# Routed expert layer, decayed attention, routed expert layer: the first layer's tiles divided 4 and 4 steps instead of 5 and 3

## The reference, cut to what matters

```python
x = x + 0.5 * ffn(layernorm(x), ...)
x = x + attn(layernorm(x), ...)
x = x + 0.5 * ffn(layernorm(x), ...)

def ffn(x, Wr, br, W1, b1, W2, b2):     # 8 experts, hidden width 512
    expert = argmax(x @ Wr.T + br)
    h = relu(x @ W1[expert].T + b1[expert])
    return h @ W2[expert].T + b2[expert]

def attn(x, ...):                       # 16 heads of 8, chunks of 128 tokens
    q, k, v = silu(x @ Wq), silu(x @ Wk), silu(x @ Wv)
    # per chunk: o = (q k^T * mask) v + lam_q * (q kv);  kv = lam_c * kv + (k * lam_k)^T v
    o = normalise(o) * gamma + beta
    return (o * sigmoid(x @ Wg1 @ Wg2)) @ Wo
```

## Time and profile before

| what | before |
|---|---|
| median of 3 runs | 430.17 us (429.95 to 430.38) |
| the profiled execution | 426.96 us |
| its span | 424.9 us |
| PE busy | 358.1 us, 84% |
| DVE busy | 288.4 us, 68% |
| POOL busy | 284.5 us, 67% |
| ACT busy | 192.1 us, 45% |
| DMA moved | 54.00 MB |

### The profile page before, as it was taken

One profiled execution on the slowest core, in us unless ns is written; L12 is line 12 of the kernel. 1 busy time (PEld: TensorE's weight loads), 2 busy tenths in 40 slices (PEclk: granted clock), 3 DMA queues, 4 the chain that ended last, 5 costly groups with the idle time before them and its releaser, 6 DMA issues.

```text
span 424.9 us, 10262 instructions
## 1 busy us (share of the span) xinstructions
PE 358.1 (84%) x2508; PEld 319.2 (75%) x2508; DVE 288.4 (68%) x995; ACT 192.1 (45%) x608; POOL 284.5 (67%) x303
## 2 busy tenths in 40 slices
PE   6788989999989979879897978855589999999920
PEld 6787879999978767667676766645489899999910
DVE  4872675444563698999898989897665676566510
ACT  5723745565546322535456363240455435555500
POOL 0027774754885999998989777620777777777770
PEclk9555999999999979998999999986599999999975
DMA  8938686887761000001010110102687846767410
GB/s 231 349 107 270 194 240 186 223 190 231 219 188 41 21 0 19 2 19 57 7 62 2 50 49 2 50 2 71 191 238 246 199 139 193 228 198 199 134 35 0
DMA packets 41303, 54.00 MB, mean 127 GB/s; under 512 B 6212, under 2 KB 25818, under 8 KB 40992
## 3 DMA queue, kind: packets, MB, share of 16 engines
q1 hardware_dynamic: 34640, 39.97, 29.9%
q0 software_dynamic: 6176, 13.26, 13.0%
q10 hardware_dynamic: 432, 0.14, 0.2%
HBM read 41.93 MB, written 12.32 MB: 128 GB/s over the span
## 4 chain that ended last, share of the span: by engine, by line
PE 55%; POOL 15%; DVE 11%; issue 10%; ACT 3%; DMA 2%; DVEq 1%; POOLq 0%; ACTq 0%
PE bank L1226 17%; PE bank L1216 17%; POOL outer_all L451 5%; PE bank L1272 4%; POOL rows L410 4%; PE bank L1176 4%; PE bank L1170 3%; POOL qS L459 3%; PE bank L1254 3%; PE bank L1208 2%; PE bank L1192 2%; POOL out_x L429 2%; PE bank L1290 2%; DVE st L702 1%; POOL kd L438 1%
## 5 line engine op out<-in xcount | busy, mean ns | idle before, releaser
L396 POOL DMA_INDIRECT ring<-rows_d,token_in x92 | 87.8, 955 | 78.0 <-DVE token_in L884 50.9
L1216 PE MATMUL bank<-slot_xT,w_ring 128*128 128x128 f32 x736 | 103.9, 283 | 4.9 <-DVE hT_b L924 4.0
L1216 PEld LDWEIGHTS bank<-slot_xT,w_ring 128*128 128x128 f32 x736 | 93.6, 197 | 8.6 <-DVE hT_b L924 6.0
L924 DVE TENSOR_SCALAR hT_b<-bank,b_cur 128x128 f32<-128x128 f32 x184 | 56.0, 346 | 38.2 <-PE bank L1216 32.6
L451 POOL TENSOR_TENSOR outer_all<-qkv 128x512 f32<-128x512 f32 x64 | 66.4, 1063 | 4.0 <-ACT qkv L577 4.0
L1272 PE MATMUL bank<-outer_all,decay_sb 128*128 128x256 f32 x256 | 68.0, 392 | 1.0 <-DVE qS L966 1.0
L560 ACT ACTIVATE hT_a<-bank,b_cur 128x128 f32<-128x128 f32 x184 | 57.3, 363 | 12.4 <-PE bank L1216 11.5
L1226 PE MATMUL bank<-w_sb,hT_a 128*128 x368 | 59.2, 284 | 3.4 <-DVE ring L937 0.6
L1272 PEld LDWEIGHTS bank<-outer_all,decay_sb 128*128 128x128 f32 x256 | 48.3, 197 | 16.6 <-issue 5.4
L1226 PE MATMUL bank<-w_sb,hT_b 128*128 x368 | 56.5, 276 | 0.0
L429 POOL DMA_INDIRECT out_x<-ring,token_out x46 | 46.1, 1002 | 14.0 <-issue 11.9
(11 more groups left out here) (127 smaller groups left out, 498.8 us busy)
## 6 DMA issues: line engine op xcount, KB each, us to landing
w_ring<-in_w1t SPq DMA_DIRECT2D x92, 256.0 KB
rows_d<-rows SPq DMA_DIRECT2D x8, 512.0 KB, 2.9
y_d<-kd SPq DMA_DIRECT2D x46, 64.0 KB
rows<-in_x SPq DMA_DIRECT2D x8, 256.0 KB, 5.9
w_sb<-in_w2t SPq DMA_DIRECT2D x1, 2048.0 KB, 8.8
rows_d<-rows SPq DMA_DIRECT2D x8, 256.0 KB, 3.7
ring<-rows_d,token_in POOLq DMA_INDIRECT x92, 4.0
decay_sb<-in_decay SPq DMA_DIRECT2D x1, 1024.0 KB, 8.1
```

The source lines that it names most:

```text
L396: pool.indirect_dma_start(n_in_ring(G) if layer_of(G) == 0 else in_ring(G), None, rows_d[u], bass.IndirectOffsetOnAxis(ap=token_in[u][:, j ...
L924: last = nc.vector.tensor_scalar(hT_b[G % 2][:, f * P:(f + 1) * P], bank_b[:, f * P:(f + 1) * P], b1_cur[G % 2][:, 2 + f:3 + f], 0.0, ALU. ...
L1216: last = mm(to[:, f * P:(f + 1) * P], w1_ring[G % W1_BUFS][:, (2 * half + f) * P:(2 * half + f + 1) * P], slot_xT[G % 2][:, :], start=True ...
```

## The change

The first layer's units get 4 and 4 steps: 16 tiles and 23 slots each. What follows from that is written out by hand: ACT's list of normalises between the routing copies, SP's store hooks (steps 4 to 7 at 6, 8, 10, 12), and GpSimd's order in attention's first five turns, with 16 fetches in place of 12, a possible fourth one in a turn ahead of half-sum 4, and four sums in place of three. The constants get one more table (`not_first16`, beside those for 12 and 20, which layer two still uses). Layer two is as it was.

```diff
-SPLIT = ((5, 3), (5, 3))
+SPLIT = ((4, 4), (5, 3))
...
-        assert SPLIT[0] == (5, 3)
+        assert SPLIT[0] == (4, 4)
...
-        BACK_IN_TURN = (2, 3, 3, 2, 2)
-        ADDED_IN_TURN = {1: SPLIT[0][0], 3: SPLIT[0][0] + 1, 4: SPLIT[0][0] + 2}
+        BACK_IN_TURN = (4, 3, 3, 3, 3)
+        ADDED_IN_TURN = {1: SPLIT[0][0], 2: SPLIT[0][0] + 1, 3: SPLIT[0][0] + 2, 4: SPLIT[0][0] + 3}
...
-            loads(0, LAYER_TILES, {0: load_attention_weights, 6: lambda: store_rows(0, 5), 8: lambda: store_rows(0, 6),
-                                   10: lambda: store_rows(0, 7)})
+            loads(0, LAYER_TILES, {0: load_attention_weights, 6: lambda: store_rows(0, 4), 8: lambda: store_rows(0, 5),
+                                   10: lambda: store_rows(0, 6), 12: lambda: store_rows(0, 7)})
...
                 half_sum(n, 3)
+                if fetches > 3:
+                    fetch_one()
                 half_sum(n, 4)
                 if fetches > 2:
                     fetch_one()
...
             for i, r in enumerate(range(first_steps, STEPS)):
-                for s in ((0,), (1, 2), (3,))[i]:
+                for s in ((0,), (1,), (2,), ())[i]:
                     normalise_tiles(s, 0, BATCH)
                 route_copy(r, r % 2, bank[r % 2])
```

## The result

The changed kernel took 434.1 us (median of 6 runs, 432.39 to 435.89) against 429.89 for the kernel before, run beside it (6 runs, 427.3 to 430.38). The ratio is 1.0105 with an interval of 1.0071 to 1.0139: 4.2 us slower by the medians and 4.5 by the ratio, where 430.5 in a range of 428.3 to 432.6 was forecast. The profiled execution took 434.58, with a span of 432.5.

What follows compares the result with a forecast made beforehand. TensorE carries over half of the chain that ended last, GpSimd and VectorE much of the rest. Terms −0.25 − 0.5 + 0.9 − 0.9 + 1.05 = +0.3, carried to the median 430.17: 430.5, range 428.3 to 432.6.

Steps and rivals of the forecast that it cites:

- First slots: Start of expert pass one: earlier loads leave quieter queues, so the first gather lands sooner; −0.5, between 0 and 1.06 gained.
- the zero end: First slots' gain of 0, the end of its range if the decay table meets the next gathers.
- Attention gets four fetches and one sum: Attention's first five turns: GpSimd's added work is partly absorbed by waits; +1.05, bounds +0.3 to +2.1.
- Routing of the first unit: Start: TensorE's queue gives away most of VectorE's saving, so the inversion of slots gains little; −0.25.
- The counts at 17: Start: a sign that the forecast is right, the first unit's counts on TensorE coming near 17.
- the start gains more: Rival at the start: inversion follows VectorE, −3.4 for −0.25, 427.3; or the clock rises a slot sooner, 428.4; chance 0.22.
- Routing of the second unit: Expert pass one: more inversion matmuls, wider VectorE operations and extra normalises between slots; +0.9, between 0.4 and 1.6.
- Fetches in the pass: End of pass one: GpSimd fetches earlier, so VectorE's 0.95 wait for the second sum goes; −0.9.
- The fetches lock: Rival in attention: each added fetch waits for the VectorE instruction beside it, 4.4 for four, 434.9; chance 0.03.
- The prediction's 15 from 620 and 3100 ns: Attention: estimate that four fetches would add some 15 at the skill's ratio; the trace showed no such growth.

Runs made afterwards that it cites:

- b_again: The kernel before, unchanged, run and profiled a second time; ratio 0.9991 to the kernel before.
- a_wlate: The changed kernel with the attention weights and decay table loaded two hooks later in SP's loop; ratio 1.0071 to the kernel before.
- a_again: The changed kernel, unchanged, run and profiled a second time; ratio 1.0107 to the kernel before.
- b_attn: The kernel before with only the changed kernel's attention schedule, its added fetches and sum using buffers nobody reads; ratio 1.0063 to the kernel before.
- a_noattn: The changed kernel without step 4's four fetches and sum in attention, leaving out part of the output; ratio 1.0052 to the kernel before.
- a_counts6: The changed kernel with the first unit's counts one step later in TensorE's queue; ratio 0.9974 to the kernel before.
- a_c6na: The changed kernel with counts one step later and without step 4's attention fetches and sum (output incomplete); ratio 0.9934 to the kernel before.
- b_wlate: The kernel before with the attention weights' load two hooks later in SP's loop; ratio 1.0003 to the kernel before.
- b_counts7: The kernel before with the first unit's counts one step later in TensorE's queue; ratio 0.9985 to the kernel before.

## Why the prediction was wrong

**The step that failed: "First slots".** It had the loads and the attention weights go up to 3 earlier (2.9 in the traces), took half of the gain that quiet queues could bring the first gather, −0.5, and put the decay table's meeting with the next gathers down as "the zero end". That end was too high: it is a loss. The first gather did not land sooner (4.4 after its issue for 3.65), and the third landed 2.6 later after its issue. From the first gather's issue to slot 2's transposes after loses 2.7 on `b_again` (−1.10 to +1.62), and `a_wlate`, which moves nothing but these loads, gains 2.0. The same is seen with a late drop: in `a_again` slot 2's transposes are 2.5 behind those of before (39.09 for 36.60), though its gathers start 0.1 earlier. The step looked at one gather and asked whether there was less ahead of it. The step should have written down, for each gather, which loads are issued ahead of it: SP's queue moved by 2.9, GpSimd's by 1.1, and the 1.5 between the third gather and the table was less than the difference.

**Right on the mechanism, the size off: "Attention gets four fetches and one sum", +1.05.** To the end of turn 2 it came as worked out: 0.7, 0.7 and 1.0 (table), with no more than a half-sum late. In all it cost 2.6 early and 3.3 late in `b_attn`, 2.0 in either kind in after less `a_noattn`, and 2.4 and 1.2 in `a_counts6` less `a_c6na`; the ratio of `b_attn` bounds it at 1.2 to 4.2. So it is about twice the forecast, at the prediction's upper bound of 2.1 rather than clearly over it. What comes after turn 2 is further lengthenings of 0.2 to 0.8 of single turns. In every kernel TensorE's granted clock falls to 0.50 (1.2 GHz) for some 4 us in a few of the turns, and most of the lengthened turns have such a stretch in them (216 to 220 and 252 to 258 in after, 194 to 198 in `b_attn`). These stretches lengthen turns with before's attention, too: from turn 2's carry products to turn 3's it takes 18.53 in `b_again`, with a stretch at 196 to 199, and 18.17 in `a_noattn`, without one; and from turn 3's to turn 4's 19.25 in `b_wlate`, with one at 214 to 218, for 18.89 in `b_again`, without one. Where and how often they come differs from one execution to the next, so how much of the loss behind turn 2 is GpSimd's and how much the clock's stays open. The long slow stretch at the head of pass two is no part of it: after, `a_again` and `b_attn` show it, but so do `b_wlate` and `a_c6na`, in which attention has before's schedule.

**"Routing of the first unit", −0.25.** About right, compared like with like: the inversion starts 0.5 earlier than in `b_again` (28.91 for 29.37) and takes 0.62 less, so the gathers start 1.1 earlier. With a late drop, which is what the prediction's rows have, they start 0.1 earlier (29.32 in `a_again`, 29.41 before). The counts at 17 hold for a late drop (17.39 in `a_again`). The cause was right, too: the queue behind the counts gives VectorE's time away. `a_counts6` shows that it could be had, 2.8 at the inversion, which the rival "the start gains more" had priced at 3.4 in all. That VectorE waits 4.14 for the inversion in after, and 1.45 in `b_again`, is the clearest sign that the engine whose work was cut no longer set the end.

**"Routing of the second unit", +0.9.** From slot 2 to slot 40 after loses 1.04 on `b_again` and 1.33 on `b_attn`, inside the 0.4 to 1.6 that it gave. GpSimd's gathers did begin later than thought, at 74.08 for 69.5 in the text: 3.4 of that is the early drop (72.04 in `b_again`, 68.69 in the earlier trace rows), the rest the first slots' loss. They were released by the tokens (`token_in`), not by the last store as forecast. No slot waited for them.

**"Fetches in the pass", −0.9.** The wait of VectorE at slot 38 went, and GpSimd waits 11.64 for qkv, as said. The size was right as well: from slot 40's transposes to slot 45's after takes 13.43, where the profiled execution of before, `b_counts7` and `b_attn` take 14.3 (`b_wlate` 13.6). Against `b_again` it is 2.44, but 1.55 of that is the slow stretch of that one execution.

**"The fetches lock", 4.4 for four:** no. Fetches in attention took 0.95 to 0.98 in after, as in before. The Trainium skill ("SBUF — State Buffer", section "SBUF: two separate sides") has GpSimd unable to write descriptors while VectorE runs in a two-port mode. No fetch here shows such a wait; that any of VectorE's instructions beside them ran in such a mode is not shown either, so the rule is not put to the test. The prediction's 15 from 620 and 3100 ns is no good estimate: under "A bandwidth-pool intuition" the Trainium skill puts the 3100 down to waiting until VectorE is done, not to a ratio.

The ledger, after less `b_again`, both early: routing −1.1, first slots +2.7, second unit's routing +1.0, end of the pass −0.9 (−2.4 with `b_again`'s slow stretch), attention +1.7, pass two +0.6 (not shown to be the change's), in all +4.0 of span (+2.5 with the slow stretch); the means of early runs, which scatter less, put the whole at 3.7. Forecast were −0.25, −0.5, +0.9, −0.9, +1.05. Two terms out of five failed, the first slots with the wrong sign and attention in its size. The other three came out near what was forecast.

## What to carry to other kernels

When a step gets shorter, list the queues in order of time with what each issue is released by, and look for pairs on different queues that swap places: here loads of 1.3 MB moved by 2.9 and got in among 64 KB gathers that moved by 1.1, and it cost 2.0, about as much as the four more fetches in attention. An in-order queue of TensorE gives no engine's saved time on unless the instruction that waits is moved too: one line, the counts one step later, was worth 3.9 early and 5.6 late in after (2.0 of it by way of the loads), and 0.9 early and nothing late in before. And take a second profile of the kernel before, if there can be one, since one execution can show a start that most don't have. The second one can have a quirk of its own, as `b_again` at slot 41: a difference between two traces is the change's only if other traces show it too.

## What the runs showed that was not expected

The start of the clock: in one execution TensorE's eight products take 0.96 at 8.11, in another of the same kernel 1.71 at 9.53, and this is worth 3.2 of 430 at the end. The granted clock of the profile doesn't show it rightly. Windows of TensorE in before (a late drop) and in `b_again` (an early one): the window, its length, TensorE's busy time with the count of its groups' matmuls, the granted clock, DMA share, GB/s.

```profile
7.00:9.00 2.00, 2.00 (x21) 1.00 1.12 360
11.00:13.00 2.00, 2.00 (x11) 0.50 1.13 367
```

```profile
7.00:9.00 2.00, 2.00 (x11) 1.00 1.10 361
11.00:13.00 2.00, 2.00 (x12) 1.00 1.16 390
```

In `b_again` 1.00 (2.4 GHz) is recorded in both, though 11 and 12 matmuls run in 2 us as in the window recorded at 0.50 (1.2 GHz) in before, and not 21. The record of an execution with an early drop has 1.00 for the whole start, which is why its mean granted clock is the higher one though it takes longer. So the duration of a known matmul tells the clock where the record is in doubt.
